# Attention heads in two row strips of TensorE, with two-part fp32r products instead of three-part bf16 ones

## What is computed

```
q, k, v = split(x @ c_attn_w + c_attn_b)            # heads of 8
scores = where(causal, q @ k.T / sqrt(8), lowest)
attn = softmax(scores)                               # heads 0, 1, 2: * mult, / sum
x = layernorm(x + (attn @ v) @ c_proj_w + c_proj_b)
h = s0 * concat(x, -x) @ (+-1);  h = relu(h) * 2
h = s1 * h @ (+-1);              h = relu(h) * 2
x = layernorm(x + s2 * h @ (+-1))
```

## Time and profile before

| | before |
|---|---|
| median of 3 runs | 921.8 us (920.85 to 927.9) |
| the profiled execution | 922.26 us, of which 919.5 us span (first to last instruction) |
| mean granted TensorE clock | 0.964 |
| busy: PE, DVE, ACT, POOL | 835.0, 621.4, 608.3, 527.3 us |
| chain that ended last, by engine | PE 60%, DVE 13%, ACT 7%, POOL 7%, issue 7%, DMA 5% |
| DMA | 53.16 MB in 65741 packets |

### The profile page before, as it was taken

How to read it: one execution, slowest core, us unless ns; L and a number is a source line. 1 busy time by engine, 2 the same in 40 slices (tenths; PEclk the granted TensorE clock), 3 DMA queues, 4 the chain that set the end, 5 groups by cost and what they waited for, 6 DMA issues and landing times.

```text
span 919.5 us, 17053 instructions
## 1 busy us (share of the span) xinstructions
PE 835.0 (91%) x5696; PEld 427.4 (46%) x5696; DVE 621.4 (68%) x2617; ACT 608.3 (66%) x1091; POOL 527.3 (57%) x763
## 2 busy tenths in 40 slices
PE   4488599999999999999999999999999999999875
PEld 1133244545455554545454554545454554545353
DVE  3487386685958587685858587685869587774124
ACT  3036267686776777676776777677776778586743
POOL 4215146575756657575756657575756658384732
PEclk9669699999999999999999999999999999999988
DMA  5735545545353545545352545545353535300000
GB/s 106 87 46 66 65 57 63 68 48 86 42 81 45 74 50 74 67 49 91 36 83 44 74 51 76 63 49 85 45 81 45 77 39 75 50 14 13 24 1 23
DMA packets 65741, 53.16 MB, mean 58 GB/s; under 512 B 5015, under 2 KB 63351, under 8 KB 65655
## 3 DMA queue, kind: packets, MB, share of 16 engines
q1 hardware_dynamic: 63542, 49.72, 39.7%
q0 software_dynamic: 960, 1.58, 1.4%
q10 hardware_dynamic: 1152, 0.79, 0.6%
HBM read 9.24 MB, written 4.19 MB: 15 GB/s over the span
## 4 chain that ended last, share of the span: by engine, by line
PE 60%; DVE 13%; ACT 7%; POOL 7%; issue 7%; DMA 5%; SPq 1%; POOLq 0%; DVEq 0%; ACTq 0%
PE av_ps L1005 11%; PE max_ps L946 11%; PE bank_ps L1032 9%; PE score_ps L970 8%; PE bank_ps L1033 7%; DVE max_ps L774 7%; PE bank_ps L929 4%; POOL res L549 3%; PE bank_ps L1080 3%; DMA stack<-parts 2%; ACT full L633 2%; ACT e L641 2%; DMA stack<-rowmaxT 2%; PE bank_ps L1047 2%; POOL rstd L539 2%
## 5 line engine op out<-in xcount | busy, mean ns | idle before, releaser
L774 DVE CUSTOM_DVE_ANT_0 max_ps<-max_ps,future 128x512 f32<-128x512 f32 (+3 forms) x1024 | 477.6, 517 | 233.9 <-PE max_ps L946 230.4
L641 ACT ACTIVATE e<-score_ps 128x512 f32<-128x512 f32 x640 | 371.3, 613 | 255.9 <-PE score_ps L970 254.6
L946 PE MATMUL max_ps<-stack 72*128 72x512 bf16 (+3 forms) x1024 | 247.6, 312 | 20.8 <-DMA stack<-parts 12.8
L970 PE MATMUL score_ps<-stack 75*128 75x512 bf16 (+3 forms) x1024 | 244.1, 303 | 17.6 <-DMA stack<-rowmaxT 10.6
L511 POOL TENSOR_SCALAR_AFFINE_SELECT e<-e 128x512 f32<-128x512 f32 x256 | 160.1, 637 | 172.2 <-ACT e L641 172.0
L519 POOL TENSOR_TENSOR h_lo<-full,h_hi 128x512 fp32r<-128x512 f32 x119 | 151.5, 1278 | 84.0 <-ACT full L633 83.9
L1005 PE MATMUL av_ps<-e,vaug 128*25 128x512 f32 (+3 forms) x2048 | 191.3, 447 | 0.0
L946 PEld LDWEIGHTS max_ps<-stack 72*128 72x128 bf16 x1024 | 81.3, 99 | 156.5 <-issue 94.0
L774 DVE DVE_READ_ACCUMULATOR2_ANT rowmax<- 128x1 f32 x1024 | 143.8, 140 | 0.0
L970 PEld LDWEIGHTS score_ps<-stack 75*128 75x128 bf16 x1024 | 91.2, 98 | 91.5 <-ACT e L641 35.0
L1032 PE MATMUL bank_ps<-h_hi,w 128*128 128x512 f32 x256 | 109.6, 428 | 0.4 <-DVE h_lo L854 0.4
(11 more groups left out here) (95 smaller groups left out, 725.8 us busy)
## 6 DMA issues: line engine op xcount, KB each, us to landing
stack<-parts SPq DMA_DIRECT2D x276, 128.0 KB
x_in<-in_L_attn_hidden_states SPq DMA_DIRECT2D x16, 256.0 KB, 15.2
x_res<-in_L_attn_hidden_states SPq DMA_DIRECT2D x16, 256.0 KB, 2.9
out_x<-res SPq DMA_DIRECT2D x16, 256.0 KB, 3.4
stack<-parts POOLq DMA_DIRECT2D x12, 128.0 KB, 12.9
stack<-rowmaxT ACTq DMA_DIRECT2D x32, 24.0 KB
e<-in_L_ffn_k SPq DMA_DIRECT2D x1, 256.0 KB, 3.3
e<-in_L_attn_c_attn_w SPq DMA_DIRECT2D x1, 128.0 KB, 2.9
```

The costliest lines, as they stand in the source:

```text
L641: nc.scalar.activation(e[g % 2][:, t, :], score_ps[:, t % 2, :], ACT.Exp, scale=SCALE).then_inc(exped, 1)
L774: return nc.vector.tensor_tensor_reduce(out=scored_block, in0=scored_block, in1=future[:, P * (T - 1 - qt):S], scale=1.0, scalar=NEG, op0= ...
L946: return nc.tensor.matmul(out_ap[:, col:col + width], st[0:QK_ROWS, h, 0, P * qt:P * qt + P], st[0:QK_ROWS, h, 1, 0:width], start=True, st ...
L970: return nc.tensor.matmul(out_ap[:, col:col + width], st[0:ALL_ROWS, h, 1, P * kt:P * kt + P], st[0:ALL_ROWS, h, 0, P * kt:S], start=True, ...
```

## The change

q and k are split into two fp32r parts instead of three bf16 ones, so there are four products of parts: 4 x 8 = 32 rows, and 35 with the maximum. Heads with an even number lie in partitions 0 to 34 of `stack` and heads with an odd number in partitions 64 to 98; `stack` is now fp32r, with 8 slots of heads instead of 16 (the same bytes per partition). The matmuls of `scores` in a group use one strip, and those of `max_scores` are reordered (`MAX_ORDER`) so that they use the other. PE's code interleaves the two: one matmul of the maxima, one of the scores, and so on (`in_turn`). In the built program a matmul's tile follows from its rows: those of 32 rows are placed in tiles of 32 x 128, at row 0 or 64; those of 35 rows in tiles of 64 x 128, at row 0 or 64; before, both were in tiles of 128 x 128.

The sums of the third block of keys move from step 5 to step 7, where the fourth is. The copies into `stack` are 8 per half and batch, of 128 KB each, in pieces of 2 KB instead of 1 KB. POOL makes the low part with one subtraction, in place; ACT's second rounding (line 716) and POOL's second subtraction (line 496) go. For batch 0 DVE does two subtractions instead of four and ACT no rounding; POOL issues ten of the copies instead of twelve. `rowmaxT` is now fp32r and lies in `x1_lo`'s memory, with two waits on DVE for that, and goes to `stack` in two DMAs (one per strip) instead of one.

```diff
-SUM_STEPS = (1, 3, 5, 7)
+SUM_STEPS = (1, 3, 7, 7)
-    QK_ROWS, MAX_ROW = 72, 72
-    ALL_ROWS = MAX_ROW + 3
+    ROW_TILE, QK_ROWS = 64, 32
+    ALL_ROWS = QK_ROWS + 3
+    def kinds(half, odd):
+        return [(half, odd, t) for t in range(STEPS)]
+    MAX_ORDER = (kinds(0, 1)[:MAX_IN_FRONT] + kinds(0, 0) + kinds(0, 1)[MAX_IN_FRONT:]
+                 + kinds(1, 0) + kinds(1, 1))
...
-        stack = [sb(f"stack{i}", [P, H, 2, S], BF16) for i in range(2)]
+        stack = [sb(f"stack{i}", [P, HALF, 2, S], F32R) for i in range(2)]
-        qk = sb("qk", [P, 2, S])
-        parts = [sb(f"parts{i}", [P, 6, S], BF16) for i in range(2)]
+        parts = [sb(f"parts{i}", [P, 4, S], F32R) for i in range(2)]
+        rowmaxT = x1_lo[0:3 * HALF, :]
...
+        def copy(eng, b, half, a, c, odd):
+            row = ROW_TILE * odd + R * (2 * a + c)
+            col = 64 * half + 32 * odd
+            return eng.dma_start(stack[b.parity][row:row + R, G * half:G * half + G, :, :].bitcast(F32),
+                                 parts[b.parity][col:col + 32, a:c + 3:c + 2 - a, :].bitcast(F32))
...
+            def split(b):
+                wait_free(pool, use_of(b, "q"))
+                wait_free(pool, use_of(b, "k"))
                 pt = parts[b.parity]
-                if k == 0:
-                    ins = nc.gpsimd.tensor_tensor(qk[:], qk[:], pt[:, 0:4:3, :], ALU.subtract)
-                else:
-                    ins = nc.gpsimd.tensor_tensor(pt[:, 2:6:3, :], qk[:], pt[:, 1:5:3, :], ALU.subtract)
+                nc.gpsimd.tensor_tensor(pt[:, 1:4:2, :], pt[:, 1:4:2, :].bitcast(F32), pt[:, 0:4:2, :].bitcast(F32),
+                                        ALU.subtract).then_inc(split_step, 1)
...
-                        elif (g, t) == MIDDLE_STEP and live(n + 2):
-                            act.wait_ge(split_step, (n + 2).times(3, 1))
-                            nc.scalar.activation(parts[n.parity][:, 1:5:3, :], qk[:], ACT.Copy).then_inc(split_step, 1)
...
+                if not half and live(b + -2):
+                    wait_full(dve, use_of(b + -2, "ffn0_3"))
...
+                                if live(n):
+                                    dve.wait_ge(rowmax_in[1], n.times(32, 32))
                                 low_part(b, 0, x1_hi[:], x1_lo[:])
...
+            def max_scores(b, i):
+                half, odd, t = MAX_ORDER[i]
+                row = ROW_TILE * odd
...
+                def part(j, qt, col):
                     width = P * (qt + 1)
+                    slot = G * half + j
+                    return nc.tensor.matmul(out_ap[:, col:col + width],
+                                            st[row:row + QK_ROWS, slot, 0, P * qt:P * qt + P],
+                                            st[row:row + QK_ROWS, slot, 1, 0:width], start=True, stop=True)
...
+            def in_turn(*programs):
+                for _ in zip_longest(*programs):
+                    pass
...
+                        steps = list(max_steps(n, g, t))
+                        for b, i in steps[:-1]:
+                            in_turn(max_scores(b, i))
+                        in_turn(*[max_scores(b, i) for b, i in steps[-1:]], *[scores(n, g, t) for _ in range(live(n))])
```

More of the change, by code:

```diff
@@ L24 @@
 from contextlib import ExitStack
+from itertools import zip_longest
 import concourse.bass as bass
@@ L522, in split_rowmax @@
             def split_rowmax(b, half):
-                m, r = rowmax[:, half], rowmax_rest[:, half]
-                hi, mid, lo = (rowmax_parts[:, half, :, i, :] for i in range(3))
+                m, r = (z[:, half].rearrange("p t (o h) -> p t o h", o=2) for z in (rowmax, rowmax_rest))
+                hi, mid, lo = (rowmax_parts[:, half, :, :, i, :] for i in range(3))
                 pool.wait_ge(max_taken, b.times(G * STEPS, 2 * STEPS * (half + 1)))
@@ L661, in rowmax_rows @@
                 wait_free(act, use_of(b, f"rowmax{half}"))
-                nc.scalar.dma_start(stack[b.parity][MAX_ROW:ALL_ROWS, HALF * half:HALF * half + HALF, 0, :],
-                                    rowmaxT[:]).then_inc(rowmax_in[half], 16)
+                for odd in range(2):
+                    row = ROW_TILE * odd
+                    nc.scalar.dma_start(stack[b.parity][row + QK_ROWS:row + ALL_ROWS, G * half:G * half + G, 0, :]
+                                        .bitcast(F32), rowmaxT[3 * G * odd:3 * G * odd + 3 * G, :].bitcast(F32)
+                                        ).then_inc(rowmax_in[half], 16)
             def iteration(n):
@@ L859, in iteration @@
                     for t in range(STEPS):
[L860 to L861 removed]
+                        for b, i in max_steps(n, g, t):
+                            take_max(b, i)
                         for what, d, _, step in places(n):
@@ L930, in transposes @@
                 last.then_inc(bank_full[u[0]], 1)
-            def max_scores(b, g, t):
-                i = STEPS * g + t
-                st, out_ap = stack[b.parity], max_ps[:, i % MAX_RING, :]
-                if t == 0 and g % 2 == 0:
-                    wait_stacked(pe, b, g // 2)
-                last_use = i - MAX_RING
-                if i < MAX_RING:
-                    last_use = max(j - G * STEPS for j in range(G * STEPS) if j % MAX_RING == i)
-                if not (b.c == 0 and last_use < 0):
-                    pe.wait_ge(max_taken, b.times(G * STEPS, last_use + 1))
-                def part(h, qt, col):
+            def max_scores(b, i):
+                half, odd, t = MAX_ORDER[i]
+                row = ROW_TILE * odd
+                st, out_ap = stack[b.parity], max_ps[:, b.times(G * STEPS, i) % MAX_RING, :]
+                if i % (2 * STEPS) == 0:
+                    wait_stacked(pe, b, half)
+                if b.times(G * STEPS, i) >= MAX_RING:
+                    pe.wait_ge(max_taken, b.times(G * STEPS, i + 1 - MAX_RING))
+                def part(j, qt, col):
```

191 lines of the change are left out of this document (82 added, 109 removed).

## The result

| | before | after |
|---|---|---|
| median | 922.3 us (4 runs) | 1797.1 us (4 runs, 1785.5 to 1810.4) |
| ratio | | 1.947 (95% interval 1.931 to 1.963) |
| span of the profiled execution | 919.5 us | 1806.9 us |
| mean granted TensorE clock of the profiled execution | 0.964 | 0.60 (0.61, 0.61 and 0.68 in the others) |
| size changes from one matmul to the next | 541 | 2303 |

The changed kernel takes almost twice as long. 877 us were forecast, with a range of 845 to 960.

A forecast was written before the change was run, and what follows sets the result against it. PE was taken to bound groups 3 and 0, DVE nearly groups 1 and 2. Overlap -1.8, visits -0.5, groups 1 and 2 -0.4: -2.7 us over fifteen iterations, -40, plus -4 at the start: 877 us, range 845 to 960.

The forecast's parts named there:

- What bounds the kernel: Steady iteration of 51.6 us: PE sets the pace in groups 3 and 0 (30.7 us), DVE nearly in 1 and 2 (20.9).
- Columns and rows: Maxima and scores on PE: 512 columns cost 0.22 us whatever the rows; overlapping strips pay once, -1.8 us an iteration.
- The weight loads: PE's loads before maxima and scores: 0.11 us each, not overlapping, so only wide steps gain, 0.22 us each.
- The changes of tile size: PE's switches between full array, column tiles and strips of 32 or 64 rows: bounds 0 and 0.12 us each, taken as 0.
- The first rival: Each change of tile size stops PE's array, up to 0.12 us: about 1110 us, or 1300 with uncovered fp32r loads; chance 0.23.
- The sign that the prediction had named for it: For drains: matmul starts 0.3 us or more apart, PE's busy time up, DVE's waits for PE far above 230 us.
- The visits: One visit fewer per group to the sums' column tiles, 0.24 us each: -0.5 us an iteration in groups 3 and 0.
- Changes between full array and strips: 18 more changes of kind (full, strip, column) in groups 3 and 0, at 0 to 0.12 us each; taken as 0.
- The second rival: Only changes between full array, strip and column cost: +0.7 us an iteration, 928 us, or 900 at half price; chance 0.15.
- The start: Batch 0's copies, up to the first maxima: earlier and fewer copies, -4 us in all, range -2 to -8.
- ACT and POOL at nothing: One ACT rounding (1075 ns) and one POOL subtraction (2134 ns) per batch go, where both have time to spare: no gain.
- the new waits on DVE at nothing: DVE's waits for x1_lo's memory cost nothing unless the maxima's DMA of step (1,2) takes some 15 us.

The follow-up runs named there:

- one_size: The changed kernel with one more row of zeros in the maxima's matmuls (33 rows), so all strips use 64-row tiles; 1025.9 us, 1.113 of the kernel before.
- rows64: The changed kernel with rows of zeros added, so that the maxima pass 61 rows and the scores 64, all in 64-row tiles; 991.6 us, 1.077 of the kernel before.

## Why the prediction was wrong, point by point

**What bounds the kernel.** PE in groups 3 and 0, DVE nearly in 1 and 2: borne out by one_size as far as it was looked at: in group 2 PE's saving turned into idle time (1.8 us of 9.08).

**Columns and rows.** "The new format costs no columns", and "if two strips work at once, the columns of two matmuls are paid once": right in one_size, where a pair of 512 starts together; overlap is worth 4.6 us an iteration there. It was not what the changed kernel runs.

**The weight loads.** Taken as 0.11 us each, one after the other, so that narrow steps would gain nothing. Wrong: loads into different strips run at the same time, and a pair of 256 columns behind another pair takes 0.12 us, half of two loads. This error went the other way.

**The changes of tile size. This is the step that failed.** The prediction counted them right, had their price in rows 4 as 0.12 us, bounded them by 0 and 0.12, and took 0, on the argument that "a load into a strip other than the one at work has no matmul in its way". Two things were wrong in it. First, the value: a change between tiles of 32 and 64 rows stops the array like any other, and the next load waits for it, whichever strip it goes to. Measured are 0.106 us in bf16, 0.20 in fp32r at the upper level and 0.30 at the lower. Second, the bound: 0.12 was read off changes next to bf16 and small loads, although the prediction had the row that shows what an fp32r load adds (304.18 to 304.52) and the loads of 99 and 192 ns. The first rival, with 1110 to 1300 us, was the right mechanism, at a chance of 0.23. The sign that the prediction had named for it is what the trace shows: starts 0.42 us apart, PE busy for 1759 us instead of 835, and DVE waiting 1011 us for PE.

The rule of the Trainium skill that the prediction quoted against the change (page "TensorEngine Tiling (Array Packing)", section "Tiling Modes": a change of tiling mode, and not just of the tile, drains TensorE, with 64-row and 32-row tiling as two modes) is what these runs show, at 0.20 us a change here; that one row of zeros is worth 771 us agrees with it. The prediction named the rule and priced the sum without it.

**The clock. Nothing in the prediction spoke of it,** though the stretches from 34 to 126 us of the kernel before were at the lower level part of the time (mean clock 0.57 from 34 to 60 us). In the changed kernel the granted clock is 0.60 on average, and the columns, the loads and the whole FFN get slower: by the estimate above that is about half of the loss, and why it was 1797 us and not the 1300 of the first rival with the load uncovered. With fewer changes the clock was higher (0.69 with 1666, 0.85 with 932, where the strips overlap as well), but 2131 changes in bf16 did not bring it down, so what lowers it is open. A rival that makes the array stop often has to be priced at both levels of the clock.

**The visits.** -0.5 us an iteration; measured alone +0.2. The visit at step 5 covered PE's wait for a bank, which appears in its place.

**Changes between full array and strips.** In fp32r they cost 0.21 us each in one_size, like the changes between strips, where 0.12 was the bound. The second rival (928 us) had this part of the mechanism at little over half the price: it has an iteration grow by 0.7 us, and in rows64, at the upper level throughout, it grew by 1.7.

**The start.** -4 us; the first maxima came 5.8 us later. The prediction looked at the copies but not at the rows of -1, whose four DMAs stand ahead of the copies and take SP 5.5 us, where two took 1.7 before. That the packets of SP's queue fall was right, but by a third and not by half: 43660 against 63542.

**ACT and POOL at nothing, the new waits on DVE at nothing:** not tested by the changed kernel, where PE fills 97% of the span and hides whatever the others do.

## What to carry to other kernels

Before putting small matmuls into strips of TensorE's rows, print the tile size of each matmul in program order and count where it changes: in this program it follows from the number of rows, and one row too few (32 instead of 33) stood between overlap and a stop at every matmul. Price each change at an uncovered weight load (here 0.10 us in bf16, 0.20 in fp32r), also those between the full array and the strips, and price the outcome at the lower clock as well if the array has to stop often. A gap on the bounding engine can be cover for someone else's latency; before removing one, look what the engine waits for next.

## What the runs showed of the hardware

- A change of tile size costs 0.106 us between bf16 matmuls and 0.20 us between fp32r ones (0.30 at the lower clock), about the load of the next weights (99 and 192 ns) plus a little. It is the same for 32 and 64 rows in bf16 (55.9 us an iteration both), and in fp32r between strips of 32 and 64 rows (0.20) as between the full array and strips (0.21).
- Two strips of one size run side by side, with their loads at the same time (both at 401.09), and a pair of 256 columns behind another pair takes 0.12 us. That holds also when the program doesn't alternate them: the second strip's matmul starts 0.01 us after the first's, ahead of an earlier instruction for the first strip.
- With the same columns the granted clock was not the same. With 33 and 36 rows in matmuls one after the other in one strip it was 0.77 and 0.85 in two runs (1205 us), with 61 and 64 rows, the added ones zeros, 0.88 and 0.91 (1089 and 1066 us); in the changed kernel the added rows did nothing (0.60 and 0.61). What it follows stays open.
- 2131 changes in bf16 with 64 and 75 rows left the clock at its upper level through the steady state.
